# All 128 steps written out, layer 1's last products ahead of the projection, the cell in PSUM and the forget gate in SBUF

## What is computed

```python
# layer 0, for each step; the first h is cond_1024, the first c is 0
a = x_t @ Wx + b + h @ Wh
i, f, o, g = sigmoid(a0), sigmoid(a1), sigmoid(a2), tanh(a3)
c = f * c + i * g
h = o * tanh(c)
x1_t = x_t + h
# layer 1, for each step; u starts as cond_1024
m = concat(x1_t, u) @ weight + bias
g = sigmoid(m0 + 1)
u = g * u + (1 - g) * tanh(m1)
out_t = x1_t + u
```

## Time and profile before

| | |
|---|---|
| median of 3 runs | 261.37 us |
| the profiled execution's own time | 261.22 us |
| its span in the profile | 259.4 us |
| TensorE matmul / weight load busy | 233.6 us (90%) / 198.4 us (76%) |
| VectorE busy | 209.6 us (81%) |
| ScalarE busy | 142.6 us (55%) |
| DMA | 7.42 MB, mean 29 GB/s |
| mean granted TensorE clock | 0.968 of full speed |

### The profile page before, as it was taken

How to read it: one execution, slowest core, us unless ns; L and a number is a source line. 1 busy time by engine, 2 the same in 40 slices (tenths; PEclk the granted TensorE clock), 3 DMA queues, 4 the chain that set the end, 5 groups by cost and what they waited for, 6 DMA issues and landing times.

```text
span 259.4 us, 14083 instructions
## 1 busy us (share of the span) xinstructions
PE 233.6 (90%) x5604; PEld 198.4 (76%) x5604; DVE 209.6 (81%) x1239; ACT 142.6 (55%) x907; POOL 5.3 (2%) x15
## 2 busy tenths in 40 slices
PE   3999999999899999999989999999999999999773
PEld 2887877877787887878878787787778787787762
DVE  5488888887888888888888888888888888888884
ACT  3455555555555555555555555555555555555552
POOL 1600000000000000000000000000000000000000
PEclk9999999999999999999999999999999999999755
DMA  6001010010101001010000101001010100000000
GB/s 205 20 14 36 23 43 14 23 44 16 43 20 30 20 20 30 20 40 13 28 29 12 38 20 40 10 20 40 10 40 20 30 20 20 14 19 15 15 3 20
DMA packets 12259, 7.42 MB, mean 29 GB/s; under 512 B 1478, under 2 KB 11980, under 8 KB 12236
## 3 DMA queue, kind: packets, MB, share of 16 engines
q1 hardware_dynamic: 11936, 6.82, 9.0%
q10 hardware_dynamic: 300, 0.28, 0.3%
HBM read 5.00 MB, written 2.10 MB: 27 GB/s over the span
## 4 chain that ended last, share of the span: by engine, by line
PE 43%; DVE 30%; ACT 13%; issue 8%; DMA 2%; POOL 2%; ACTq 0%; POOLq 0%; DVEq 0%
PE a L282 9%; PE fo L257 8%; ACT late_bank L410 7%; DVE cell L492 6%; DVE h_high L499 6%; DVE pair L511 5%; DVE acts L515 5%; PE a L273 4%; PE ig L257 4%; DVE scan_add L486 4%; PE fo L262 3%; PE ig L228 3%; ACT acts L416 3%; PE fo L228 3%; PE a L233 3%
## 5 line engine op out<-in xcount | busy, mean ns | idle before, releaser
L257 PE MATMUL fo<-h_high,wh_part 128*128 128x32 f16 x762 | 59.3, 179 | 16.7 <-DVE h_high L499 10.4
L257 PEld LDWEIGHTS fo<-h_high,wh_part 128*128 128x128 bf16 x762 | 36.5, 97 | 29.5 <-DVE h_high L499 27.6
L262 PE MATMUL fo<-h_low,wh_part 128*128 128x32 f16 x508 | 52.9, 180 | 0.0
L400 ACT ACTIVATE late_bank<-fo 128x32 f32<-128x32 f32 x128 | 23.3, 182 | 46.8 <-PE fo L262 46.1
L273 PE MATMUL a<-h_high,w1x_part 128*128 128x32 f16 x768 | 45.1, 177 | 1.0 <-DVE h_low L504 0.9
L415 ACT ACTIVATE acts<-a 128x64 f32<-128x64 f32 x128 | 28.4, 222 | 26.1 <-PE a L282 26.1
L499 DVE SCALAR_TENSOR_TENSOR h_high<-out_gate,late_bank 128x32 f16<-128x32 f32 x128 | 24.0, 187 | 23.1 <-ACT late_bank L410 17.8
L406 ACT ACTIVATE out_gate<-fo 128x32 f32<-128x32 f32 x128 | 25.2, 197 | 30.7 <-PE fo L262 30.7
L276 PE MATMUL a<-h_low,w1x_part 128*128 128x32 f16 x512 | 41.9, 177 | 0.0
L282 PE MATMUL a<-acts,w1h_part 128*128 128x32 bf16 x768 | 40.3, 179 | 0.1
L257 PE MATMUL ig<-h_high,wh_part 128*128 128x32 f16 x762 | 38.4, 177 | 0.0
(11 more groups left out here) (79 smaller groups left out, 445.9 us busy)
## 6 DMA issues: line engine op xcount, KB each, us to landing
xT<-in_x_dram SPq DMA_DIRECT2D x16, 128.0 KB, 2.1
x_add<-in_x_dram SPq DMA_DIRECT2D x32, 64.0 KB, 1.8
out_dram<-outT SPq DMA_DIRECT2D x32, 64.0 KB, 1.6
wx_s<-in_L_cond_Wx_dram SPq DMA_DIRECT2D x1, 256.0 KB, 3.1
wh_raw<-in_L_cond_Wh_dram ACTq DMA_DIRECT2D x1, 256.0 KB, 3.6
w_raw<-in_L_cond_weight_dram SPq DMA_DIRECT2D x1, 256.0 KB, 4.1
bias_rows<-in_biases_dram ACTq DMA_DIRECT2D x1, 3.0 KB
condT<-in_cond_dram ACTq DMA_DIRECT2D x1, 16.0 KB, 4.2
```

What stands on the lines that cost most here:

```text
L257: nc.tensor.matmul(gate_step(q, j), wh_part[:, w, q * P:(q + 1) * P], h_high[:, (j - 1) % PARTS, :], start=False, stop=False, skip_group_c ...
L262: mm = nc.tensor.matmul(gate_step(q, j), wh_part[:, w, q * P:(q + 1) * P], h_low[:, (j - 1) % PARTS, :], start=False, stop=w == 1, skip_gr ...
```

## The change

There are three parts.

The hardware loop goes: TensorE, ScalarE, VectorE and the DMA queue's program are all written out over 128 steps, and semaphore values become constants.

On TensorE the two `u_low` products move ahead of the step's piece of projection.

The cell becomes columns of a PSUM bank of its own. `tanh_c` gets a PSUM bank of its own too. The forget gate goes to an SBUF tile.

```diff
-        cell = sb("cell", [P, N, 2])
+        forget = sb("forget", [P, N])
...
-        late_bank = bank("late_bank")
-        forget, tanh_c = late_bank[:, 0:N], late_bank[:, N:2 * N]
+        cell_bank, tanh_bank = bank("cell_bank"), bank("tanh_bank")
+        cell = cell_bank[:, 0:2 * N].rearrange("p (n two) -> p n two", two=2)
+        tanh_c = tanh_bank[:, 0:N]
...
-        def schedule(eng, body):
-            body(0, True, False)
-            with eng.Fori(BODY, T - BODY, BODY) as s0:
-                body(s0, False, False)
-            body(T - BODY, False, True)
+        def schedule(body):
+            for s0 in range(0, T, BODY):
+                body(s0, s0 == 0, s0 == T - BODY)
...
-            groups(0, False)
-            with sp.Fori(1, GROUPS // 2 - 2) as b0:
-                groups(b0 * 2, False)
+            for g0 in range(0, GROUPS - 4, 2):
+                groups(g0, False)
...
                         layer1_rest(r, l)
+                        layer1_low(r, l)
                     if more:
                         if k == 0:
...
                             bias1(other)
-                    if not (first and j == 0):
-                        layer1_low(r, l)
...
-            def body(s0, first):
+            for s0 in range(0, T, BODY):
                 for j in range(BODY):
-                    if not (first and j == 0):
+                    if s0 + j:
                         hidden(s0 + j - 1, (j - 1) % BODY)
-                    until_cell(s0, j, first)
-
-            body(0, True)
-            with dve.Fori(BODY, T - BODY, BODY) as s0:
-                body(s0, False)
-            body(T - BODY, False)
+                    until_cell(s0, j, s0 == 0)
```

More of the change, by code:

```diff
@@ L364, in body @@
                             bias1(other)
-                    if not (first and j == 0):
-                        layer1_low(r, l)
-            schedule(pe, body)
+            schedule(body)
             pe.wait_ge(acts1_ready, T - 1)
@@ L425, in body @@
                         layer1(s - 1, (j - 1) % BODY)
-            schedule(act, body)
+            schedule(body)
             layer1(T - 1, BODY - 1)
```

## The result

The changed kernel took 250.43 us (median of 4 runs, 248.91 to 251.54) against 261.15 before (4 runs, 260.88 to 261.54). The ratio is 0.9584, with an interval of 0.9528 to 0.964. In a later round it was 0.9522 (0.9487 to 0.9557), with a median of 249.28 (6 runs). The profiled execution took 248.91 with a span of 247.1. The forecast was 248.4, with a range of 245.0 to 254.5.

A forecast was written before the change was run, and what follows sets the result against it. The projection was taken to delay the u_low products, ScalarE's layer 1 and pair in each step. The move's 12.3 us (writing out included) plus 0.6 for the memories made 12.9 less: 248.4 us, range 245.0 to 254.5.

The forecast's parts named there:

- the wait's 0.15: VectorE's extra delay from h_low to pair behind a projection, waiting for ScalarE; 0.13 us of it stays in the step.
- The cover: TensorE's spare time between the moved projection's end and the next step's first weight load: about 0.1 us.
- rival B: Projection now delays h_high's products on TensorE: 88 steps grow, 2.6 to 4.4 us in all, 251 to 253; 13 in 100.
- E: The new TensorE order moves nothing, ScalarE's layer 1 being ready no sooner: 261 us, within 0.5; 2 in 100.
- One sign: In steps with projection, the waits of TensorE's load for h_high should be short, near 0.1 us.
- the 0.15 that the prediction counted in B's favour: Before the change, TensorE's weight load waited for h_high only 0.15 us in a step with projection.
- 0.4 us inside the sum: Writing out the loop's steps removes VectorE's waits for issue: some 0.4 us, already counted in the 12.3 us gain.
- Rival D: Instruction fetch shows on the engines: 39 new packets at 0.35 us cost 13.7 us, time 262.1; 3 in 100.
- the nothing that I took from the memset: VectorE's scan writing PSUM was taken as no longer than writing SBUF, with bounds of 20 ns either way.
- Rival A: VectorE's scan into PSUM is slow: 0.06 us more in 125 intervals, 7.5 us, time 255.9; 12 in 100.
- C: The PSUM part reaches its best bound, 4.4 us more gain than taken: 244.0 us; 5 in 100.
- the memories' 0.6: Cell in PSUM and forget gate in SBUF: tanh 20 ns shorter, gate 15 longer, over 125 intervals 0.6 us less.

The follow-up runs named there:

- before_pad512: The kernel before, with a 512-column product of zeros added between the projection and the u_low products: 280.75 us, ratio 1.0739.
- memories_only: The kernel before with only the cell moved to PSUM and the forget gate to SBUF, loop and order as before: 261.1 us, ratio 0.9983.
- move_only: The kernel before with only the two u_low products moved ahead of the projection, loop and memories as before: 250.5 us, ratio 0.9586.
- all_but_memories: The changed kernel with the cell back in SBUF and forget gate and tanh in one PSUM bank: 249.38 us, ratio 0.9554.
- the warm kernels: Kernels with ten products of zeros added on TensorE ahead of the first projection; the changed kernel with them: 248.97 us, ratio 0.9516.

## Why the prediction was right, and where it was off

*What bounds the kernel.* Right in substance: the projection kept back the `u_low` products, ScalarE's layer 1 and `pair`. The runs sharpen it. I wrote that the wait's 0.15 stays in the step with 0.13, as if it were added to the chain of layer 0. It is a ring of its own, all in layer 1, that takes 1.95 us a turn, and layer 0 was waiting for it: 0.22 us put into it came out in full (before_pad512), and changes to scan and `tanh` did nothing to it (memories_only). That the step fell to 1.82 and no further is layer 0's own chain, as predicted.

*The move.* Right: all steps went to 1.82. 11.4 us of the steps' 12.8 come with the move alone. The cover was put at 0.1; 0.11 were free, and of 0.22 0.13 were, so rival B did not happen, and neither did E. One sign did not come: TensorE's load was to wait only near 0.1 for `h_high` behind a projection, and it waits 0.32 in the step shown. The loads of the projection's weights are done 0.3 us before `h_high` releases the next ones (at 103.83, against 104.15), while the product itself still runs until 104.24, so this wait doesn't measure the cover, and the 0.15 that the prediction counted in B's favour said little.

*Writing out.* I gave it 0.4 us inside the sum, from the two waits that the view lists. It lists only the long ones: the later turns of the loop had short waits too, which is seen in move_only, in two intervals of each turn. In the steps it was 0.6 alone, 1.2 with the move (move_only against all_but_memories) and 0.4 with move and warm-up. I had costed the start at nothing, and there it loses about 0.5. Its worth for the kernel's time is small and not settled: alone it is 1.0028; with the move the medians of the same round are 1.1 us apart, with runs that overlap; in the warm kernels the ratios are 0.9516 against 0.9514 across rounds, and 0.9493 against 0.9514 within one, where the memories differ too. Rival D didn't occur in the steps.

*The memories.* The durations of ScalarE came as read from the rows, 182 and 198. The scan grew by 13 ns, inside the bounds of 20 but not the nothing that I took from the memset. Together with `tanh` and the gate that leaves an interval as it was; I had -5 ns and so 0.6 us, and the runs show between 0.2 us for the part (229.4 to 229.2) and 0.1 against it (warm, 229.4 to 229.5). By the figures of the Trainium skill (Perfetto Trace Analysis, Optimizing Scalar/DVE Operations) the scan would have grown by an estimated 65 ns; the trace shows 13 for this form. Rival A falls, as does C.

*The sum.* From the third `h_high` to the last it was 239.9 before and is 242.2 - 14.81 = 227.4 now, 12.5 us less; forecast were 12.9, and the difference is the memories' 0.6 less some rounding. Four terms that I had put at nothing nearly cancel. The second interval also fell to 1.82, 0.2 less, and the first from 2.44 to 2.32. The tail behind the last `h_high` fell from 5.3 to 4.9; why wasn't tried. Against them the first `h_high` comes 1.0 later: half of it are the later weights (4.9 against 4.4), and in the rest TensorE was still slow, with the full clock from 8.7 against 7.2: of the first eight projection products the last two took 1.06 us against 0.67 before. So the profiled execution is at 248.91 against 248.3 by the sum, and that it is so close is in part luck. What makes the median 250.43 lies, as far as is known, outside all steps of my sum, in the run's start. This is shown by the five profiles above, one of them slow, and by the scatter that shrank with ten products of zeros, not by a profile of a slow run of the changed kernel itself.

*The best version.* No variant is clearly ahead of the changed kernel's good runs. With the warm-up products and the cell in SBUF the median is 248.79 and the runs lie within 0.5 us; without the products it is 249.28 to 250.43.

## What to carry to other kernels

Look for rings: a product that signals another engine should not stand behind independent work in its queue, however small it is; what is between the last input's release and that signal is paid in full, while the same work behind it was free here, the 0.51 of the projection and up to 0.13 more. A step of the same kernel that lacks the suspected work, here the last eight, gives the price of removing it without any run. Compare the spread of the runs before and after as well as their medians, and look at the first microseconds when it grows.

## What was unexpected in the hardware

The same three products in the first step took 1.85 us in one profile and 0.94 in another, with the same inputs, by the moment at which TensorE's clock rose: the full level began 2.8 us after the first product in the kernel before and 9.4 us after it in move_only. With ten products of zeros ahead of them the runs of a kernel lie within 0.5 to 0.7 us, against 1.2 to 2.9 for the fast kernels without.

At the end the granted clock falls to 0.50 (from 234.0 us in the changed kernel), and the last four steps, which have no projection, take 1.84 in place of 1.82 us: half the clock cost them 0.02.

VectorE's scan of 64 elements took 300 ns writing PSUM and 287 writing SBUF.

The first weights (256 KB) landed 2.9 to 3.3 us after their issue in the six profiles with the loop and 3.5 to 4.3 us in the eight that were written out.
